# Tokens through a buffer in memory with one load per chunk, queries and keys loaded from SyncE's queue, and a new order

## The reference

```python
def tok(img, ...):                       # 64 images, 196 patches of 768 numbers
    x = layernorm(patches(img), ln1_g, ln1_b)
    return layernorm(x @ W + b, ln2_g, ln2_b)

h = concatenate([tok(x), txt], axis=1)   # 64 x 273 x 256
...
Q, K, V = proj(Wq, bq), proj(Wk, bk), proj(Wv, bv)     # of layernorm(h)
scores = einsum('nqhd,nkhd->nhqk', Q, K) * scale
out = einsum('nhql,nlhd->nqhd', softmax(scores), V)
h = h + out.reshape(n, s, e) @ Wo.T + bo               # 16 heads of 16, per image as the kernel groups them
...
xr, xk = mixes of z and z one token before, z = layernorm(h)
h = h + sigmoid(xr @ W_r.T) * (relu(xk @ W_k.T) ** 2 @ W_v.T)
```

## Time and profile before

| | us |
|---|---|
| median of three runs | 1717.25 |
| lowest, highest | 1715.13, 1725.07 |
| the profiled execution | 1719.71 |
| its span, first to last instruction | 1718.0 |
| PE busy in the span | 1442.6 |
| DVE, ACT, POOL busy | 1244.6, 1128.1, 910.5 |

### The profile page before, as it was taken

One profiled execution on the slowest core, in us unless ns is written; L12 is line 12 of the kernel. 1 busy time (PEld: TensorE's weight loads), 2 busy tenths in 40 slices (PEclk: granted clock), 3 DMA queues, 4 the chain that ended last, 5 costly groups with the idle time before them and its releaser, 6 DMA issues. The chain is left out here.

```text
span 1718.0 us, 51431 instructions
## 1 busy us (share of the span) xinstructions
PE 1442.6 (84%) x17678; PEld 1353.0 (79%) x17678; DVE 1244.6 (72%) x3109; ACT 1128.1 (66%) x2410; POOL 910.5 (53%) x1593
## 2 busy tenths in 40 slices
PE   3587898898799888989898898987989879898866
PEld 3577888798788877888887888887888878787755
DVE  5477887787668777868787787776777677786543
ACT  3456686677577677767666776776666667676554
POOL 2231475456555455556564665555544656556356
PEclk8688999899899889999999999998989999998988
DMA  5178687779677778768878887678778587868650
GB/s 132 40 145 144 152 153 117 148 156 142 126 122 149 132 132 147 150 122 146 150 125 152 138 153 152 127 144 136 132 139 137 120 133 132 149 130 125 119 79 28
DMA packets 676232, 225.56 MB, mean 131 GB/s; under 512 B 591051, under 2 KB 647175, under 8 KB 675975
## 3 DMA queue, kind: packets, MB, share of 16 engines
q1 hardware_dynamic: 392615, 186.09, 53.2%
q10 hardware_dynamic: 283360, 36.18, 19.0%
HBM read 119.28 MB, written 90.05 MB: 122 GB/s over the span
## 5 line engine op out<-in xcount | busy, mean ns | idle before, releaser
L1771 PE MATMUL bank<-wqkv,xnT 128*128 128x384 f32 x1656 | 352.5, 359 | 15.8 <-DVE xnT L1571 14.9
L1771 PEld LDWEIGHTS bank<-wqkv,xnT 128*128 128x128 f32 x1656 | 299.1, 200 | 21.5 <-DVE xnT L1571 16.8
L1875 PE MATMUL bank<-wtok,xT 128*126 128x258 f32 (+1 forms) x1800 | 267.8, 308 | 0.0
L1668 ACT ACTIVATE arena<-qk,ymask 128x384 f32<-128x384 f32 x368 | 199.5, 608 | 81.1 <-DMA qk<-qkv_dram 42.7
L1875 PEld LDWEIGHTS bank<-wtok,xT 128*126 128x126 f32 (+1 forms) x1800 | 249.0, 209 | 0.0
L1400 POOL TENSOR_TENSOR mixp<-mixf,mixp 128x384 fp32r<-128x384 f32 x184 | 184.2, 1014 | 86.0 <-ACT mixp L1747 85.9
L1376 POOL TENSOR_TENSOR hb<-hc,bob 128x768 f32<-128x768 f32 x46 | 84.4, 1835 | 190.3 <-DVE h L1594 180.9
L1580 DVE TENSOR_TENSOR qkvt<-bank,bqkv 128x384 f32<-128x384 f32 x276 | 149.7, 546 | 29.2 <-PE bank L1771 28.1
L1689 ACT ACTIVATE xcols<-xim 84x640 f32<-84x640 f32 (+1 forms) x192 | 126.8, 695 | 47.5 <-DVE xs L1506 26.8
L1698 ACT ACTIVATE xT<-bank 128x420 fp32r<-128x420 f32 (+14 forms) x285 | 104.2, 419 | 62.7 <-PE bank L1856 46.4
L1344 POOL TENSOR_TENSOR rs<-ve,small 126x1 f32<-126x1 f32 (+1 forms) x192 | 134.4, 700 | 15.1
(11 more groups left out here) (119 smaller groups left out, 3339.1 us busy)
## 6 DMA issues: line engine op xcount, KB each, us to landing
qkv_dram<-qkvt SPq DMA_DIRECT2D x138, 384.0 KB
xim<-in_x SPq DMA_DIRECT2D x128, 294.0 KB
qk<-qkv_dram ACTq DMA_DIRECT2D x46, 768.0 KB, 10.5
arena<-qkv_dram SPq DMA_DIRECT2D x368, 48.0 KB
out<-h SPq DMA_DIRECT2D x45, 384.0 KB, 3.9
o_dram<-probs SPq DMA_DIRECT2D x108, 96.0 KB, 2.3
on<-o_dram SPq DMA_DIRECT2D x73, 128.0 KB
o_dram<-probs SPq DMA_DIRECT2D x88, 48.0 KB, 2.0
```

What stands on the lines that cost most here:

```text
L1668: kb_sb.done(A.activation(kb[:, :, yy, :].rearrange("p (a u) k -> p a u k", u=UNITS), qk[:, :, HD:2 * HD].rearrange("p (a u) k -> p a u k" ...
L1771: ins = mm(psum, left(a, k), right(b, k), start=t == 0, stop=t == len(terms) - 1)
L1875: ins = mm(place("tok", 0, t)[0:pr, 0:E + 2], xT[:, a, ch, :, :].rearrange("p i w -> p (i w)")[:, r0:r0 + pr], wtok[:, b, ch, :], start=n ...
```

## The change

**Tokens.** A new buffer `h_dram` in memory holds all tokens. The text is copied into it by four DMAs of 16 images each (1.26 MB). A patch tile is copied from `yh` to `h_dram` in one or two DMAs, cut at images only: 156 in all. A new step `hin` loads a chunk's 384 rows into `hc` in one DMA (the last chunk in two); it takes over the waits for the free slot, and waits on SP for the last four tiles' copies and for the text's. `st3` waits for this load alone.

**Queries and keys.** `qk_in` moves from ScalarE's program to SyncE's, with its waits.

**Small things.** `row_pieces` calls `spread` with 16 in place of 9 (256 DMAs in place of 259). `st2` waits for `mv2` of the tile before, and `st3` for `mv3` of the chunk before.

**Order.** `AT` and `BANK` are new for all steps. The diff, cut to its core; the tables show their first row only:

```diff
+TIMG = 16
...
 AT = dict(
     load=[
-        [5, 14, 28, 54, 93, 139, 185, 259, 389, 439, 535, 685, 773, 884, 1055, 1193, 1280, 1400, 1589, 1672,
+        [6, 14, 28, 54, 93, 127, 174, 220, 312, 347, 433, 603, 705, 789, 836, 985, 1188, 1293, 1463, 1596,
...
 def patch_pieces(t):
 
-    out = []
-    for a, b in cut(PT * t, PT * t + patch_rows(t), [PATCHES]):
-        shift = (T - PATCHES) * (a // PATCHES)
-        for lo, hi in cut(a + shift, b + shift, [TT]):
-            for at, rows in spread(lo, hi - lo, 32):
-                out.append((at - shift - PT * t, rows) + place_of(at))
-    return out
+    first = PT * t
+    return [(a - first, b - a, a + (T - PATCHES) * (a // PATCHES))
+            for a, b in cut(first, first + patch_rows(t), [PATCHES])]
...
-            for lo, hi in cut(CT * c, min(CT * c + CT, TOKENS), [TT, T]) for at, rows in spread(lo, hi - lo, 9)]
+            for lo, hi in cut(CT * c, min(CT * c + CT, TOKENS), [TT, T]) for at, rows in spread(lo, hi - lo, 16)]
...
+        h_dram = nc.dram_tensor("h_dram", (TOKENS, E), F32, kind="Internal").ap()
...
-                for m in due(s, "txt", 0):
-                    c = text_pieces(m)[-1][2]
-                    after(xn_sb, c - SLOTS, 3)
-                    after(hb_sb, c - SLOTS, 1)
-                    for t0, rows, cc, i, p in text_pieces(m):
-                        text_in.done(m, sp.dma_start(hc[p:p + rows, cc % SLOTS, i, :],
-                                                     txt[m:m + 1, t0:t0 + rows, :].rearrange("b t e -> (b t) e")))
+                for n in due(s, "txt", 0):
+                    dst = h_dram.rearrange("(b t) e -> b t e", t=T)[TIMG * n:TIMG * n + TIMG, PATCHES:T, :]
+                    text_out.done(n, sp.dma_start(dst, txt[TIMG * n:TIMG * n + TIMG, :, :]))
                 for t in due(s, "hdma", 0):
-                    c = patch_pieces(t)[-1][2]
-                    after(xn_sb, c - SLOTS, 3)
-                    after(hb_sb, c - SLOTS, 1)
                     after(h_sb, t, 1)
-                    for t0, rows, cc, i, p in patch_pieces(t):
-                        patch_in.done(t, sp.dma_start(hc[p:p + rows, cc % SLOTS, i, :], yh[t0:t0 + rows, t % 2, :]))
+                    for first, rows, at in patch_pieces(t):
+                        patch_out.done(t, sp.dma_start(h_dram[at:at + rows, :], yh[first:first + rows, t % 2, :]))
+                for k in due(s, "hin", 0):
+                    after(xn_sb, k - SLOTS, 3)
+                    after(hb_sb, k - SLOTS, 1)
+                    for t in chunk_tiles(k)[-4:]:
+                        after_all(patch_out, t)
+                    after_all(text_out, chunk_images(k)[-1] // TIMG)
+                    if OUT_ROWS[k] == CT:
+                        rows_in.done(k, sp.dma_start(hc[:, k % SLOTS, :, :], h_dram[CT * k:CT * k + CT, :].rearrange("(i t) e -> t i e", t=TT)))
...
+                for k in due(s, "qk_in", 0):
+                    after_all(qkv_out, k)
+                    after(kb_sb, k - 1, 4 * PARTS)
+                    after(q_sb, k - 1, 2 * PARTS)
+                    src = qkv_dram[k % SLOTS, :, :, 0:2 * HD]
+                    qk_in.done(sp.dma_start(qk[:, :, :], src.rearrange("(g t) i j -> (t i) g j", t=8)))
...
+                    mv2_sb.wait(dve, t - 1, 1)
                     y_sb.wait(dve, t, 1)
...
-                    patch_in.wait(dve, t - 2)
+                    patch_out.wait(dve, t - 2)
...
+                        mv3_sb.wait(dve, k - 1, i + 1)
                         if i == 0:
-                            for t in chunk_tiles(k)[-4:]:
-                                patch_in.wait(dve, t)
-                            for m in chunk_texts(k):
-                                text_in.wait(dve, m)
+                            rows_in.wait(dve, k)
...
-                for k in due(s, "qk_in", 0):
-                    qkv_out.wait(act, k)
-                    settle(act)
```

More of the change, by code:

```diff
@@ L764 @@
+        [int(b) for b in "7161454117146517266014416152076166761604101031"],
     ],
     qkv=[
[L766 to L772 removed]
@@ L905 @@
 PATCH_DMAS = [len(patch_pieces(t)) for t in range(PTILES)]
-TEXT_DMAS = [len(text_pieces(m)) for m in range(IMAGES)]
 ROW_DMAS = [len(row_pieces(c)) for c in range(CHUNKS)]
@@ L918, in chunk_tiles @@
 def chunk_tiles(c):
-    return [t for t in range(PTILES) if any(piece[2] == c for piece in patch_pieces(t))]
-def chunk_texts(c):
-    return [m for m in chunk_images(c) if any(piece[2] == c for piece in text_pieces(m))]
+    lo, hi = CT * c, CT * c + OUT_ROWS[c]
+    return [t for t in range(PTILES) if any(at < hi and at + rows > lo for first, rows, at in patch_pieces(t))]
 class Signal:
@@ L1650, in _ @@
                     square_weight(n)
-                for k in due(s, "qk_in", 0):
-                    qkv_out.wait(act, k)
-                    settle(act)
-                    if k > 0:
-                        kb_sb.wait(act, k - 1, 4 * PARTS)
-                        settle(act)
-                        q_sb.wait(act, k - 1, 2 * PARTS)
-                        settle(act)
-                    src = qkv_dram[k % SLOTS, :, :, 0:2 * HD]
-                    qk_in.done(act.dma_start(qk[:, :, :], src.rearrange("(g t) i j -> (t i) g j", t=8)))
                 for part in range(PARTS):
```

81 lines of the change are left out of this document (43 added, 38 removed), and 1097 rows, old and new, of tables (add, av, carry, d).

## The result

| | us |
|---|---|
| before, median of four runs beside it | 1721.16 (1715.13 to 1728.22) |
| changed, median of four runs | 1605.72 (1593.35 to 1617.08) |
| ratio | 0.9326, 95% interval 0.9245 to 0.9407 |
| the profiled execution of the changed kernel | 1607.39, span 1605.3 |

The account below looks back on a forecast made before the run. PE was taken as the bound in the middle, with 169 us idle. Start +17, chunk 0's rows +2, middle -45 and end -9 summed to -35: 1684.7 us, 1682 against the median, range 1645 to 1735.

Parts of the forecast that it names:

- The bound: Middle, 200 to 1600 us: PE busy 1231 of 1400 us, so 169 us of idle PE for an order to win.
- I let a third come back: -45 us: Middle: 68 us of PE's waits for `on` should go, a third returns elsewhere; ends 0 and -68.
- waits that I named as next in line: Middle: `zt` of the chunk before, the values' load and the image loads were expected to be late next.
- The surplus of PE's work ahead of each load: PE's work beyond SP's before `on` loads: mean 6.7 us before, 10.9 now; need 8; shortfalls fall from 96 to 27.
- rival A: Middle and end: all computed shortfalls go and queries and keys land in 7 us; -63, 1654 us; chance 0.12.
- SP's work: SP's issues: fewer patch and text copies, some new ones; net 101 to 166 us less, mid 143.
- Rows through memory: Token path 2 to 5 us longer per chunk, hidden in the middle, paid once for chunk 0: +2 us.
- Queries and keys in SP's queue: Moving their load to SP: bounds 3.5 us gain in landing to 7.0 us of SP held per chunk; taken as zero.
- rival B: SP's queue is held behind the load of queries and keys, the middle gains nothing; +26, 1743 us; chance 0.18.
- DMA at no cost under a share of 0.85: Middle: 0.39 MB more per chunk, 8% of the bytes, costed at nothing while the share stays under about 0.85.
- The start: Text copies ahead of images 0 and 1 delay image 1, leaving 12 to 24 us of delay; taken as +17.
- The end: Last three chunks: more PE work between the last `qkv` and the scores; -9 us, between 0 and -14.

Follow-up runs that it names:

- a_xact: Changed kernel with the loads of images 2 to 63 begun by ScalarE in place of SP: 1640.27 us.
- a_qkact: Changed kernel with the load of queries and keys begun by ScalarE again, at the same place of the order: 1657.63 us.
- a_hin: Changed kernel with each chunk's load moved up to right behind the last copy it needs and the freeing of its slot: 1690.91 us.
- a_load8: Changed kernel with eight 1 KB copies that nothing reads added on SP ahead of each load of `on`: 1801.72 us.
- b_tok_qk: Kernel before, in its old order, with tokens through memory and the load of queries and keys on SP: 1773.77 us.
- b_load3: Kernel before with three 1 KB copies that nothing reads added on SP ahead of each load of `on`: 1788.68 us.
- load experiments: Small unused 1 KB copies added to SP's program per chunk, in the changed kernel and the one before: 1675.51 to 1801.72 us.
- b_tok: Kernel before, in its old order, with tokens through memory, each chunk's load right behind the last copy it needs: 1739.34 us.
- a_load3: Changed kernel with three 1 KB copies that nothing reads added on SP ahead of each load of `on`: 1675.51 us.
- b_qk: Kernel before with only the load of queries and keys moved to SP, at its old step: 1741.44 us.
- b_nosettle: Kernel before without the semaphore increments behind SP's waits, which nobody waits for: 1702.05 us.

## Why the prediction was wrong

**The bound.** "So PE is the bound there, and 169 us of idle PE are what an order can win" was half of it. What an order can win is the idle time and what that idle time does to the clock. The wait of 8.2 us from the prediction's, cut out of the trace of the kernel before:

```profile
598.00:606.00 8.00, 8.00 (x71) 7.96 (x71) 4.92 (x14) 6.50 (x13) 6.23 (x16) 1.00 0.36 103
606.00:614.80 8.80, 0.62 (x6) 0.38 (x4) 4.22 (x7) 1.38 (x5) 2.41 (x6) 0.65 1.14 157
614.80:618.00 3.20, 3.18 (x15) 3.19 (x16) 1.58 (x3) 2.10 (x5) 0.63 (x1) 0.50 0.44 47
618.00:622.00 4.00, 4.00 (x27) 4.00 (x26) 2.99 (x8) 3.25 (x8) 3.84 (x7) 0.89 1.03 94
```

PE was busy at a clock of 1.00 up to the wait (2.4 GHz), it fell in the wait, and the first 3.2 us of work after it ran at 0.50 (1.2 GHz): 15 matmuls in 3.2 us, where the next stretch has 27 in 4. The Trainium skill describes this in TensorE: Matmul & The Clock Gate, Part 1: The HAM clock gate (the "warmup" mystery), as a gate between these two levels that activity opens; the trace agrees, 1.00 before and 0.50 right after. I had the row of 0.94 in hand and made no term of it. Over the whole run, in which all kernels have the same matmuls, it reads:

| kernel | order | PE idle, us | PE busy, us | clock |
|---|---|---|---|---|
| changed | new | 205.8 | 1399.5 | 0.951 |
| a_xact | new | 230.8 | 1411.9 | 0.945 |
| a_qkact | new | 244.9 | 1419.2 | 0.935 |
| a_hin | new | 264.8 | 1424.2 | 0.931 |
| a_load8 | new | 337.2 | 1458.6 | 0.908 |
| before | old | 275.4 | 1442.6 | 0.921 |
| b_tok_qk | old | 316.8 | 1450.1 | 0.920 |
| b_load3 | old | 331.5 | 1454.0 | 0.908 |

From before to after, 69.6 us less of idle came with 43.1 us less of busy time. The small copies of a_load8, which touch nothing of PE's work, make the changed kernel idle for 131 us more and busy for 59 us more: waits that are put in slow the same matmuls. In the old order the copies of b_load3 cost 56 us of idle and only 11 of busy, so it isn't one price per us. The number of long waits doesn't settle it either. In the middle 26 waits of PE were over 2.5 us before and 6 are after, but b_load3 has 36. What sets the price is open.

**"I let a third come back: -45 us".** Too much. The wait for `on` fell by 81.5 us, to 13.7 where 27 were computed and 20 to 45 forecast. PE's idle time fell by 71.0, past the upper end of -68, so some 10 us came back elsewhere. Of the waits that I named as next in line two did grow: at the products with the values from 3.0 to 20.3 us, and at `zt` (L1908) from 0.9 to 9.7. Others fell, for `xs` from 16.5 to 5.3 us and for `xnT` from 11.2 to 1.7, and made up for most of it. The surplus of PE's work ahead of each load was the right evidence; the third was a rule of thumb. The objection to rival A, that PE would be at 93%, was none: it was at 92.1% (1186.2 of 1288.06).

**SP's work.** Right in its prices per median issue (0.391 for the patches' copy, in the bounds of 0.35 to 0.77), wrong in the sum: 47 us of relief in place of 143. Issues of over 3 us grew from 17 with 63 us to 43 with 221 us, 41 of them next behind `qk_in`. Its place in the argument was off as well. The load experiments show 0.79 us of time for each added us of SP in the kernel before already, where I had made SP's lateness one cause of the waits for `on` alone. But that price doesn't hold for relief by another path or queue: in three such experiments SP had 82 to 148 us less of issues, and the time did not fall.

**Rows through memory, "hidden in the middle".** Right in the changed order, where SP waits 9.0 us for the landings (in 200 to 1500), but only because of the order. With the same copies back to back it costs 103 to 106 us of SP over the run (a_hin, b_tok, b_tok_qk). "Nothing" was the price of the edit and the place together, and I gave no row for the distance between a copy and its load.

**Queries and keys in SP's queue, "I take zero".** The mechanism of rival B is there: single issues of SP behind `qk_in` last over 4 us in 36 of 46 chunks, which was half of its sign. Its other half, a wait for `on` of 80 us or more, is not, nor its price: the move costs 20 us in the old order and is worth 52 in the new. Zero failed as well. The reason given for it, that SP had paid for the collision before, holds only in small part, for the issues of the values fell from 366 to 346 us alone. The landing of 8.3 us was inside the forecast's bounds, 7.0 to 10.5.

**DMA at no cost under a share of 0.85.** It went to just 0.85 and 158 GB/s. That the fuller engines cost nothing is not shown: issues that the change left alone took longer, those of the images 87 us in place of 57 and the stores of `qkvt` 75 in place of 55, held ones among them.

**The start.** The mark of chunk 1 came 25.5 us later against +19, but for another reason: only 7.9 us are idle time of PE, which the forecast was about, and 17.6 are work moved ahead of the mark. In b_tok, in the old order and with the same 1412 matmuls ahead of the mark, it came 21.4 us later. Image 1 at 39.50 against "40 to 52", image 0 at 22.23 against "25 to 33": the stretch from 10 to 20 us, in which text and image 0 arrive, moved 311 GB/s where it had moved 176, so the delay lies at the fast end of what I computed, or just beyond it.

**The end.** -7.6 against -9. Right, and by the mechanism forecast: PE's waits of 14.5 us for queries and keys from 1600 on the earlier trace rows are 0.7 us in the changed kernel's end (from 1500).

Taken together: two terms failed. The one for the clock was missing (-43 us of busy time over the run), and a third was taken off the idle time of the middle (-26 us). The idle time of the start, 7.9 in place of 19, gives another -11, and the end took 2 or 3 back. That is the 78 us between -35 and -112.7.

**What stays open.** How the 168 us of the order divide. The distance of the chunk loads from their copies is one part, 85 us by a_hin. The rest may go with other distances in PE's program (ahead of the transposes of the probabilities, of `wo`, and of `zt`), which were not changed one by one. It isn't settled either what makes a second queue dear for the images, nor why time added to SP costs that much, while the relief of b_tok, a_qkact and a_xact gave nothing back.

## What to carry to other kernels

Find out what added time in an engine's program costs before you price edits to it: three small transfers per round, put in on purpose, showed in one run that a us of SyncE cost 0.8 us, which PE's busy share of 88% had hidden. Don't turn the number round: where issues were taken off SyncE by way of another queue or path, its waits grew instead. An edit of data flow that is worth nothing in the old order can pay in a better one, as the load of queries and keys did (20 us lost, 52 won), so price the two together, and look above all at how far a load stands behind the store that it must wait for. And when waits of several us before TensorE go away, count its clock as well: here that gave 43 us beside the 70 of the waits themselves.

## What the runs showed of the hardware

- A copy of 1 KB from memory to memory took SP 0.55 to 0.60 us to issue in the median (a_load8, a_load3), more than a store of 128 rows of 3 KB (0.35, `qkvt`).
- The issue next behind a load of 768 KB in SP's queue took 4.5 us in the median and up to 7.8 (changed kernel), 4.8 in b_qk; in the kernel before, with the load in ScalarE's queue, two issues of the whole run took over 4 us. The DMA share was 1.34 in one of 7.34 us.
- The load of 768 KB of queries and keys landed in 7.9 to 8.6 us in the median when SP began it beside everything else, and in 9.8 to 11.0 when ScalarE did, in either order.
- Four copies of 1.26 MB from memory to memory landed in 7.8 to 13.5 us.
- An increment of a semaphore behind each wait of SP costs 1.2% in the kernel before (b_nosettle).
